# Attention scores from two 16-bit parts of q and k, 48 rows, on two row halves of TensorE

## The reference

```
x = x + 0.5 * ffn(layernorm(x))
x = x + attn(layernorm(x))
x = x + 0.5 * ffn(layernorm(x))
ffn(x):  gate, up = split(x @ ternary(w_gate_up).T)        # 2 x 2048 columns
         h = rms_norm(silu(gate) * up);  return h @ ternary(w_proj).T
attn(x): Q = x @ Wq.T + bq  (32 heads of 16);  K, V: 8 heads of 16
         Q, K = rope(Q), rope(K);  4 query heads share one K and V head
         w = softmax(Q @ K.T / 4);  return (w @ V) @ Wo.T + bo
```

## Time and profile before

| | |
|---|---|
| median of three runs | 3522.47 us |
| span of the profiled execution, first to last instruction | 3517.8 us |
| its own time (page of the profile) | the span; what lies around it is not on the page |
| TensorE, VectorE, ScalarE, GpSimd busy | 92%, 61%, 49%, 27% |
| ternary weights and first FFN | 0 to about 900 us |
| projections | about 900 to 1150 us |
| opening maxima of attention | 1150 to 1189 us |
| attention blocks | 1189 to 2660 us |
| output projection, second FFN | 2660 to 3518 us |

### The profile page before, as it was taken

How to read it: one execution, slowest core, us unless ns; L and a number is a source line. 1 busy time by engine, 2 the same in 40 slices (tenths; PEclk the granted TensorE clock), 3 DMA queues, 4 the chain that set the end, 5 groups by cost and what they waited for, 6 DMA issues and landing times. The chain is left out here.

```text
span 3517.8 us, 53208 instructions
## 1 busy us (share of the span) xinstructions
PE 3248.7 (92%) x16160; PEld 1283.3 (36%) x16160; DVE 2155.8 (61%) x2674; ACT 1710.1 (49%) x3188; POOL 933.6 (27%) x788
## 2 busy tenths in 40 slices
PE   1189999999888899999999999999998899999999
PEld 0144444444454122222222222222223344444444
DVE  9934333332577888888888888888872344333332
ACT  4434333332122377777777777777772033333332
POOL 6826444444455000000000000000002245444443
PEclk9999999999999799999999999999999999999999
DMA  3300111101334111111111111111124601100001
GB/s 96 101 34 11 39 37 41 44 33 37 87 108 122 26 36 35 34 31 35 35 33 33 32 31 35 35 35 34 33 81 153 215 13 36 36 36 36 36 24 36
DMA packets 186527, 178.06 MB, mean 51 GB/s; under 512 B 62800, under 2 KB 123472, under 8 KB 186448
## 3 DMA queue, kind: packets, MB, share of 16 engines
q1 hardware_dynamic: 186448, 177.04, 17.1%
HBM read 123.99 MB, written 52.43 MB: 50 GB/s over the span
## 5 line engine op out<-in xcount | busy, mean ns | idle before, releaser
L1149 DVE TENSOR_REDUCE at_neg_max<-at_max_ps 128x1 f32<-128x1024 f32 x1024 | 1206.1, 1219 | 227.8 <-PE at_max_ps L1039 227.7
L1139 ACT ACTIVATE at_probs<-at_score_ps 128x512 f32<-128x512 f32 x2048 | 1057.9, 603 | 348.5 <-PE at_score_ps L1057 348.5
L1039 PE MATMUL at_max_ps<-at_km,at_q 96*128 96x512 bf16 x2048 | 625.8, 387 | 15.5 <-PEq L634 9.3
L1057 PE MATMUL at_score_ps<-at_q,at_ks 98*128 98x512 bf16 x2048 | 629.1, 382 | 7.3 <-ACT at_probs L1139 5.5
L1064 PE MATMUL at_out_ps<-at_probs,at_v 128*32 128x512 f32 x4096 | 545.5, 605 | 0.1
L350 DVE TENSOR_TENSOR f_h<-f_gate,f_up_ps 128x512 f32<-128x512 f32 x256 | 175.7, 687 | 592.0 <-ACT f_gate L433 571.8
L1329 POOL TENSOR_TENSOR rows<-rows,bias 128x512 f32<-128x512 f32 x32 | 39.4, 1266 | 1601.1 <-ACTq L1268 1518.1
L433 ACT ACTIVATE f_gate<-f_gate_ps 128x512 f32<-128x512 f32 x256 | 153.0, 597 | 602.2 <-PE f_up_ps L521 602.2
L521 PE MATMUL f_gate_ps<-f_xt_hi,wt 128*128 128x512 f16 x1024 | 394.0, 385 | 22.3 <-DVE f_h L350 13.1
L483 POOL TENSOR_TENSOR f_sqsum<-f_sqsum,f_sq 128x512 f32<-128x512 f32 x224 | 283.8, 1267 | 424.0 <-ACT f_sq L440 422.1
L549 PE MATMUL f_out_ps<-wt,f_h_hi 128*128 128x512 bf16 x1024 | 390.1, 381 | 5.5 <-DVE rows L374 5.5
(11 more groups left out here) (92 smaller groups left out, 2577.7 us busy)
## 6 DMA issues: line engine op xcount, KB each, us to landing
rows<-x SPq DMA_DIRECT2D x40, 1024.0 KB, 5.7
at_q<-qk_parts SPq DMA_DIRECT2D x384, 64.0 KB, 2.1
x<-rows SPq DMA_DIRECT2D x16, 1024.0 KB, 5.1
tw_raw<-units SPq DMA_DIRECT2D x48, 256.0 KB, 2.6
rows<-x SPq DMA_DIRECT2D x32, 256.0 KB, 3.0
at_q<-at_max_parts SPq DMA_DIRECT2D x512, 1.0 KB
att<-at_out SPq DMA_DIRECT2D x256, 32.0 KB
ao_a<-att SPq DMA_DIRECT2D x8, 1024.0 KB
```

The source lines that it names most:

```text
L1039: last = nc.tensor.matmul(max_ps[u % 2][:, half * QB:(half + 1) * QB], q[k][0:SROWS, j, h * QB + c * P:h * QB + (c + 1) * P], km[k][:, hal ...
L1057: nc.tensor.matmul(score_ps[pos % RING][:], ks[k][:, kc * P:(kc + 1) * P], q[k][:, j, h * QB:(h + 1) * QB], start=True, stop=True).then_in ...
L1139: nc.scalar.activation(probs[:, kc % PBUF, j, :], score_ps[pos % RING][:], ACT.Exp, scale=HD ** -0.5).then_inc(exps, 1)
L1149: nc.vector.tensor_reduce(neg_max[:, h, u:u + 1], max_ps[u % 2][:], AX.X, ALU.max, negate=True).then_inc(maxed, 1)
```

## The change

q and k are split into two float16 parts instead of three bfloat16 parts, and the product has three terms of 16 rows, 48 in all, or 50 with the two rows of the maxima. Heads 0 and 2 of a group lie on partitions 0 to 49, heads 1 and 3 on 64 to 113; keys lie on both halves. Scores are taken in the order 0, 2, 1, 3, and one max matmul of a head of the other half follows each score. The rows against the maxima hold 2^14 (`ANCHOR`), and the maxima are divided by it; they are filled by four DMAs, once. In the projections the rest, mid and GpSimd's low part fall away: VectorE writes the low part itself. A new class `Balance` scales the weights and biases of queries and keys by inverse powers of two, so that both have like sizes, during the first tile of the first FFN. `qk_parts` has two parts, and the waits on the stores follow.

```diff
class Balance:                      # new; its buffers and semaphores are left out here
    def measure_queries(self, dve):
        dve.wait_ge(self.w_in, W_DMAS * 16)
        w, b = self.parts[0]        # w_qkv[:, :, 0:FQ] and its bias; parts[1]: FQ:FA
        dve.tensor_reduce(self.largest[:, 0:1], w, AX.XY, ALU.max, apply_absolute_value=True).then_inc(self.measured, 1)
    def measure_rest(self, dve):    # the same for the keys' weights and for the two biases
...
    def total_over_rows(self, pe, ps):
        pe.wait_ge(self.measured, 4)
        pe.matmul(ps[:, 0:4], self.ones, self.largest[:], start=True, stop=True).then_inc(self.summed, 1)
    def take_factors(self, dve, ps):   # nine operations on 1 to 4 columns, each waits for the one before
...
    def apply(self, dve, k):
        dve.wait_ge(self.factors, 1)
        for part in self.parts[k]:
            dve.tensor_scalar(part, part, self.factor[:, k:k + 1].bitcast(F32), None, ALU.mult)
...
 # ffn, VectorE, gate_up, behind hidden(t, c), in f1 only
+                    if balance and isinstance(t, int) and t == 0:
+                        if c == 1: balance.measure_queries(dve)
+                        if c == 2: balance.measure_rest(dve)
+                        if c == 6: balance.take_factors(dve, out_ps[2])
+                        if c == 9: balance.apply(dve, 0)
+                        if c == 10: balance.apply(dve, 1)
 # ffn, TensorE, gate_up
+                    if balance and isinstance(t, int) and t == 0 and c == 4:
+                        balance.total_over_rows(pe, out_ps[2])
...
 # projections
-                for n, part in enumerate((high, mid, low)):
+                for n, part in enumerate((high, low)):
...
-                nc.vector.tensor_tensor(rest[:, k % 2], feat_ps[:, 0:NF, :],
-                                        high[:, k // 2 % 2, :, (k % 2) * P:(k % 2 + 1) * P],
-                                        ALU.subtract).then_inc(rests, 1)
+                nc.vector.tensor_tensor(low[:, k // 2 % 2, :, cols], feat_ps[:, 0:NF, :],
+                                        high[:, k // 2 % 2, :, cols], ALU.subtract).then_inc(lows, 1)
...
-            steps(pool, NSUB, [(0, root), (3, sine), (5, low_part)], unroll=RX, peel=RX)
+            steps(pool, NSUB, [(0, root), (3, sine)], unroll=RX, peel=RX)
...
-            steps(act, NSUB, [(2, copy_turned), (5, high_part), (5, mid_part)], unroll=RX, peel=RX)
+            steps(act, NSUB, [(2, copy_turned), (5, high_part)], unroll=RX, peel=RX)
...
 # attention
-TERMS = ((0, 0), (0, 1), (1, 0), (1, 1), (0, 2), (2, 0))
+TERMS = ((0, 0), (1, 0), (0, 1))
+SLOT = P // 2
+SLOTS = P // SLOT
+ANCHOR = 2.0 ** 14
+ORDER = (0, 2, 1, 3)
+UNITS = [(2 * (u // 8) + 1 - u % 2, u // 2 % 4) for u in range(MU)]
-Q_DMAS = K_DMAS = len(TERMS)
+Q_DMAS = K_DMAS = len(TERMS) * SLOTS
...
-        self.q = [sb(f"q{k}", [KROWS, GH, T], BF16) for k in range(2)]
-        self.km = [sb(f"km{k}", [SROWS, T], BF16) for k in range(2)]
-        self.ks = [sb(f"ks{k}", [KROWS, T], BF16) for k in range(2)]
+        self.q = [sb(f"q{k}", [P, GH // SLOTS, T], F16) for k in range(2)]
+        self.km = [sb(f"km{k}", [P, T], F16) for k in range(2)]
+        self.ks = [sb(f"ks{k}", [P, T], F16) for k in range(2)]
...
 # SP, load_q: one DMA for each term and slot (load_k likewise)
+            for slot in range(SLOTS):
+                r0 = slot * SLOT + s * HD
+                sp.dma_start(self.q[k][r0:r0 + HD, :, h * QB:(h + 1) * QB],
+                             src.rearrange("(i o d) t -> o d i t", o=SLOTS, d=HD)[slot]).then_inc(self.q_in[k][h], 16)
 # SP, once, ahead of the first store_max
+            sp.wait_ge(ones_set, 1)
+            for k in range(2):
+                for slot in range(SLOTS):
+                    row = slot * SLOT + SROWS
+                    sp.dma_start(ks[k][row:row + 2, :], anchor[:]).then_inc(anchor_in, 16)
...
 # TensorE, maxima
+                j, c = UNITS[u]
+                rows = slice(j % SLOTS * SLOT, j % SLOTS * SLOT + SROWS)
+                if half == 0:
+                    after(pe, maxed, m * MU + (u - 1))
+                done = nc.tensor.matmul(max_ps[u % 2][:, half * QB:(half + 1) * QB],
+                                        q[k][rows, j // SLOTS, h * QB + c * P:h * QB + (c + 1) * P],
+                                        km[k][rows, half * QB:(half + 1) * QB], start=True, stop=True)
 # TensorE, scores
+                unit, j = kc * GH + i, ORDER[i]
+                rows = slice(j % SLOTS * SLOT, j % SLOTS * SLOT + KROWS)
-                nc.tensor.matmul(score_ps[pos % RING][:], ks[k][:, kc * P:(kc + 1) * P],
-                                 q[k][:, j, h * QB:(h + 1) * QB], start=True, stop=True).then_inc(s_done, 1)
+                nc.tensor.matmul(score_ps[pos % RING][:], ks[k][rows, kc * P:(kc + 1) * P],
+                                 q[k][rows, j // SLOTS, h * QB:(h + 1) * QB], start=True, stop=True).then_inc(s_done, 1)
 # TensorE, run
-                            scores(n, k, h, kc, j, turned)
-                            if j % 2 == 1 and ahead:
-                                ahead.pop(0)()
+                            scores(n, k, h, kc, i, turned)
+                            if follow >= 1:
+                                maxima(n + NB, 1 - k, h, kc * MSTEP + i // 2, i % 2)
...
 # VectorE, split_maxima
-                nc.vector.tensor_copy(max_parts[:, h, 0, :], ps[0:MU, 0:P]).then_inc(m_high, 1)
+                nc.vector.tensor_scalar(max_parts[:, h, 0, :], ps[0:MU, 0:P], 1.0 / ANCHOR, None,
+                                        ALU.mult).then_inc(m_high, 1)
...
+            nc.vector.memset(anchor[:], ANCHOR).then_inc(ones_set, 1)
             for k in range(2):
-                nc.vector.memset(ks[k][SROWS:KROWS, :], 1.0).then_inc(ones_set, 1)
```

More of the change, by code:

```diff
@@ L224, in ffn @@
+def ffn(nc, name, rows, x_in, stored, src, before, dst, wt, ident, ones, neg_half, start_next, balance=None):
     x = rows[:, 0:SUB, :]
@@ L651, in projections @@
         sind = sb("sind", [P, 2, FA], F32)
[L652 to L655, removed]
+        high = sb("high", [P, 2, NF, 2 * P], F16)
+        low = sb("low", [P, 2, NF, 2 * P], F16)
         turn_ps = [bank(f"turn_ps{k}", [P, DC, P]) for k in range(2)]
@@ L839, in features @@
                 pe.wait_ge(roped, i + 1)
-                after(pe, rests, i)
+                after(pe, lows, i)
                 for c in range(NF):
@@ L1032, in _, with maxima @@
             pe.sem_inc(pv_done, PBUF)
-            def maxima(m, k, h, u):
-                j, c = u // (QB // P), u % (QB // P)
-                after(pe, maxed, m * MU + (u - 1))
-                for half in range(T // QB):
-                    last = nc.tensor.matmul(max_ps[u % 2][:, half * QB:(half + 1) * QB],
-                                            q[k][0:SROWS, j, h * QB + c * P:h * QB + (c + 1) * P],
-                                            km[k][:, half * QB:(half + 1) * QB], start=True, stop=True)
-                last.then_inc(m_done, 1)
+            def maxima(m, k, h, u, half):
+                j, c = UNITS[u]
[5 more added lines that the diff above has]
+                                        km[k][rows, half * QB:(half + 1) * QB], start=True, stop=True)
+                if half == T // QB - 1:
+                    done.then_inc(m_done, 1)
             def turn_maxima(m, h, ps):
@@ L1074, in _ @@
                         turn_maxima(0, 0, score_ps[0])
-                    maxima(m, 0, m, u)
-            pe.wait_ge(ones_set, 4)
+                    for half in range(T // QB):
+                        maxima(m, 0, m, u, half)
+            pe.wait_ge(ones_set, 3)
+            pe.wait_ge(anchor_in, 2 * SLOTS * 16)
             def run(G, k, before, follow):
@@ L1132, in run @@
                         act.wait_ge(pv_done, n * KC + (kc + 1))
-                        for j in range(GH):
-                            unit = kc * GH + j
+                        for i, j in enumerate(ORDER):
+                            unit = kc * GH + i
                             pos = unit + (unit >= TURN_POS)
@@ L1391, in start_projections @@
                 pj_load(sp, i, i)
-        ffn(nc, "f1", rows, f_in[0], f_stored[0], x, [], x1, wt, ident, ones, neg_half[:], start_projections)
+        balance = Balance(nc, ctx, w_qkv, bias, w_in, ones)
+        ffn(nc, "f1", rows, f_in[0], f_stored[0], x, [], x1, wt, ident, ones, neg_half[:], start_projections, balance)
         with ExitStack() as outer:
```

127 lines of the change are left out of this document (94 added, 33 removed).

## The result

The changed kernel takes 3283.9 us (median of 4 runs, 3280.9 to 3301.2) and the kernel before 3523.5 us (4 runs, 3522.5 to 3530.1): a ratio of 0.9327, 95% interval 0.9304 to 0.9351. Forecast were 3295 us, 11 us more.

A forecast was written before the change was run, and what follows sets the result against it. Attention was taken as largest, with TensorE setting its pace and VectorE 16% behind. Gains of 199 (attention), 28 (projections) and 1 (opening) less 1 (Balance) made 227 us, so 3522.5 - 227 = 3295 us; 80% range 3265 to 3390.

The forecast's parts named there:

- Overlap of the row halves, pairs of 0.22: Attention: scores and max matmuls in different row halves overlap, four pairs taking 0.87 us a step in place of 1.74.
- Plain step 2.41, by the ring's loop: Attention: the fourth score waits for the first exponential through the three-bank score ring; step 2.41 us, from 2.83.
- Copy step 2.60: Attention step with the output copy: first exponential starts 0.19 us later, the fourth score follows it; 2.60 us.
- Turn step 2.69: Attention step turning the maxima: third score waits for the split behind a VectorE reduction; 2.61 to 2.7, taken 2.69 us.
- Block 19.75, 199 us: Attention: six plain steps, one copy and one turn step make 19.75 us, from 22.96; 62 blocks gain 199 us.
- VectorE's floor 19.41: Attention: sixteen reductions of 1.177 us plus 0.58 for two small splits limit a block to 19.41 us (220 us gained).
- Rival 4: Everything meets its floor, block 19.41 us and projections gaining 33 us: 3268 us in all; chance 8%.
- Changes of tiling at no new cost: Attention: a step still changes twice between tiling modes of TensorE, so nothing new was charged.
- SP's chain at nothing: Attention: SP's DMA chain, 18.7 us, just fits the shorter block; charged 0, bound 0.5 us every second block, 15 us.
- Projections 28 us: Projections: without GpSimd's low part the rotate falls from 1.93 to 0.83 us, tile 7.66 to 6.73; 28 us, bounds 0 to 33.
- Opening 1 us, Balance -1: Opening maxima gain 1 us from one memset fewer; Balance's VectorE work in the first FFN tile costs 1 us.
- The sum: Whole kernel: 199 + 28 + 1 - 1 = 227 us gained, from 3522.5 to 3295 us.

The follow-up runs named there:

- the two runs with other orders: Changed kernel with max matmuls on the preceding score's own row half, 3418.1 us; changed kernel with both max matmuls after every second score, 3424.3 us.
- the halves of the weighing: Changed kernel with the weighing cut into two 256-column halves, the second one step later between second and third score: 3240.2 us.
- 3224.9: Kernel with the weighing in halves, plus SP's six max-key loads moved behind the max-row stores: 3224.9 us, ratio 0.9153 to the kernel before.
- three kernels: Changed kernel, 3283.9 us; the same with exponentials on 256 of 512 columns, 3249.5 us; the same with the weighing in halves, 3240.2 us.

## Why the prediction was right

- **Overlap of the row halves, pairs of 0.22.** Right, by the rows of the plain step: 0.22 for a pair of different halves, and in the two runs with other orders 0.22 for each matmul where two of one half follow each other. The prediction did not see what makes the order matter, which is the wait of the fourth score.
- **Plain step 2.41, by the ring's loop.** 2.39. The mechanism is shown by the halved reductions, which change nothing, and by the halves of the weighing, which hide it.
- **Copy step 2.60.** 2.59.
- **Turn step 2.69.** 2.60, but the reason given was wrong. The prediction let the fourth score follow the third by 0.22 and the third wait for the split, and then took 2.69 where its own sum ended at 2.61. In the rows of the turn step the third score starts 0.99 after the turn and not 1.07, and the fourth is held by the first exponential instead. The step is the plain 2.39 plus the 0.21 that the turn takes ahead of the first score. That 1.07 + 0.22 and the end of that exponential both fall on 1.29 is luck.
- **Block 19.75, 199 us.** 19.61, and 210 us by 62 x 3.39. Of the 11 us missed, 9 are these 0.14 us a block (62 x 0.14); the rest is that 22.96 for the old block, the steady loop's, was 23.00 on the mean. Against the steady 19.56 the 19.75 are 0.19 too much, 0.10 from six plain steps and 0.09 from the turn step.
- **VectorE's floor 19.41.** Wrong, without effect on the sum: it was the opening's pace, taken for a limit. 18.7 was reached. Rival 4, all at the floor, was therefore no lower bound; 3224.9 lies 43 us below it.
- **Changes of tiling at no new cost.** Right: 0.32 and 1.00 stand as in the earlier trace rows. What the draining rule costs ("TensorEngine Tiling (Array Packing)", Key Properties, in the Trainium skill) is small here, if the whole of the following is that drain, which no run separates: a half weighing costs 0.09 ahead (0.31 for 0.22) and 0.12 behind (0.57 for half of the 0.89) however short it is.
- **SP's chain at nothing.** Right at 19.61, and its bound was real: it held every second block at 18.7.
- **Projections 28 us.** 32.6. The rotate did what was said. Two terms were off, and in part they cancelled. The old tile was 7.49 from rotate to rotate in most of the trace; the 7.66 of the earlier trace rows is one of six long ones in 31. The new tile is 6.38 and not 6.73, which was the sum of features, turn and products and left out that they overlap by 0.35. So a tile gained 1.11, what the rotate lost, and the upper bound of 33 was nearly reached. The shared port of "SBUF — State Buffer" (Who interferes with whom, in the Trainium skill) is borne out by the run with GpSimd's extra subtraction: 2.07 in place of 0.83.
- **Opening 1 us, Balance -1.** 1.4, and nothing.
- **The sum.** 227 us were predicted, and 245 gained where the change is, so the terms were 18 us too small together. The medians differ by 240, and by the ledger the rest was lost in stages that vary from profile to profile. That the total came out 11 us from the forecast rather than 18 is luck.

## What to carry to other kernels

Two row halves of TensorE worked side by side here, and it started a matmul on the free half ahead of an earlier one on the busy half. What the order of the stream decided is what stood behind the score that waits for its exponential: one max matmul of the other half cost nothing, one more, or one of the same half, cost 0.22 us a step and more, 134 to 140 us of the 237. So look first at what stands behind a wait. When the engine that sets the pace gets faster, look for loops through a ring of buffers before looking at the busiest engine: a ring of three is hidden only by work that stands within three places, and halving a long operation to put it there gave 44 us, where moving the whole cost 23. Then read the DMA queue's order; it was the next limit, at a cost of six moved lines.

## What the runs showed of the hardware

- Two 512-column matmuls on partitions 0 to 49 and 64 to 113 ran in the time of one (0.22 us a pair at full clock), without a wait of one half's weight loads on the other. Two of one half took 0.22 us each.
- With two scores of one half ahead of two max matmuls of the other in the stream, the first max matmul started 0.01 us after the first score and 0.22 before the second, in all 220 steps looked at: between halves, TensorE did not keep the order of the stream.
- VectorE without idle time between reductions was not at its limit: the same sixteen took 19.11, 18.62 and 18.28 us in three kernels, with 1.22 us for each in all. The start-to-start distance, not the duration or the idle time, told how near it was.
- A GpSimd subtraction beside VectorE's rotate made that 2.07 us long in place of 0.83, on operands of its own.
